# Row maxima turned in blocks by VectorE and DMA, an earlier front and masks first, in a two-layer attention kernel

## What is computed

```python
# block 0, with H = 32 heads of D = 16
xn = _layernorm(x)
qkv = xn @ qkv_w + qkv_b                      # 512 -> 3 * 512
q, k = _rope(q, cos, sin), _rope(k, cos, sin)
scores = einsum('bhqd,bhkd->bhqk', q, k) * scale + (1 - causal) * MASK_VAL
s = (softmax(scores) @ v) @ out_w + out_b
g = silu(xn @ W_gate.T) * (xn @ W_up.T) @ W_down.T      # 512 -> 1376 -> 512
x = x + s * silu(g)
# block 1
xn = _layernorm(x)
s = recurrent net of width 64 (4 layers: long convolution, mlp of 256), 512 -> 64 -> 512
g = silu(oct(xn, w_gate)) * oct(xn, w_up), through oct(., w_down)   # ternary octonion weights
x = x + s * silu(g)
```

## Time and profile before

| what | value |
|---|---|
| time, median of 3 runs (lowest to highest) | 611.6 us (611.2 to 612.4) |
| time of the profiled execution | 611.91 us |
| its span | 610.0 us |
| granted TensorE clock, mean | 1.000 |
| busy: PE, PEld | 590.7 us (97%), 424.7 us |
| busy: DVE, ACT, POOL | 383.0, 290.2, 386.2 us |
| DMA | 83.63 MB, 137 GB/s in the mean |

### The profile page before, as it was taken

One profiled execution on the slowest core, in us unless ns is written; L12 is line 12 of the kernel. 1 busy time (PEld: TensorE's weight loads), 2 busy tenths in 40 slices (PEclk: granted clock), 3 DMA queues, 4 the chain that ended last, 5 costly groups with the idle time before them and its releaser, 6 DMA issues.

```text
span 610.0 us, 9847 instructions
## 1 busy us (share of the span) xinstructions
PE 590.7 (97%) x3368; PEld 424.7 (70%) x3368; DVE 383.0 (63%) x912; ACT 290.2 (48%) x448; POOL 386.2 (63%) x598
## 2 busy tenths in 40 slices
PE   6999999999999999999999999999999999999996
PEld 5876666666677887666666666788887676767664
DVE  5986778666427489877786663366985261516257
ACT  3625777556734622276766566354122453232432
POOL 6896956656435578878575555348979594821363
PEclk9999999999999999999999999999999999999999
DMA  9788776654512237658577554942600000000002
GB/s 302 236 303 251 208 212 189 195 139 103 145 54 87 87 103 220 210 165 250 148 216 223 154 160 130 353 157 95 238 5 1 1 0 2 0 1 1 0 30 109
DMA packets 60369, 83.63 MB, mean 137 GB/s; under 512 B 17936, under 2 KB 26768, under 8 KB 60320
## 3 DMA queue, kind: packets, MB, share of 16 engines
q1 hardware_dynamic: 57968, 75.02, 41.2%
q10 hardware_dynamic: 2352, 8.00, 3.4%
HBM read 65.17 MB, written 26.99 MB: 151 GB/s over the span
## 4 chain that ended last, share of the span: by engine, by line
PE 79%; DMA 5%; DVE 3%; issue 3%; POOL 3%; ACT 3%; SPq 2%; POOLq 0%; ACTq 0%; DVEq 0%
PE proj_ps L1004 9%; PE proj_ps L1006 7%; PE proj_ps L1005 7%; PE ctx_ps L1161 5%; PE score_ps L1034 4%; PE proj_ps L1209 4%; PE proj_ps L1210 3%; PE scoreT_ps L1043 3%; PE score_ps L1004 2%; PE score_ps L1006 2%; PE score_ps L1005 2%; PE scoreT_ps L1004 2%; PE scoreT_ps L1006 2%; PE scoreT_ps L1005 2%; PE ctx_ps L1209 2%
## 5 line engine op out<-in xcount | busy, mean ns | idle before, releaser
L821 POOL TENSOR_TENSOR w_lo<-raw,w_hi 128x512 fp32r<-128x512 f32 x98 | 132.3, 1355 | 64.7 <-ACT w_hi L1374 59.2
L1555 DVE CUSTOM_DVE_ANT_0 score_ps<-score_ps,causal 128x512 f32<-128x512 f32 (+3 forms) x256 | 118.9, 522 | 60.7 <-PE score_ps L1034 60.5
L1423 ACT ACTIVATE probs_T<-scoreT_ps 128x1024 f32<-128x1024 f32 x80 | 82.2, 1027 | 46.1 <-PE scoreT_ps L1043 45.0
L1004 PE MATMUL proj_ps<-xn_hi,w_hi 128*128 128x512 f32 x224 | 96.8, 432 | 1.6 <-ACT by_sin L1352 1.2
L1006 PE MATMUL proj_ps<-xn_lo,w_hi 128*128 128x512 f32 x224 | 88.5, 395 | 0.0
L1005 PE MATMUL proj_ps<-xn_hi,w_lo 128*128 128x512 f32 x224 | 88.5, 395 | 0.0
L852 POOL TENSOR_SCALAR_AFFINE_SELECT probs_T<-probs_T 128x256 f32<-128x256 f32 x128 | 55.5, 457 | 14.2 <-ACT probs_T L1423 14.1
L1004 PEld LDWEIGHTS proj_ps<-xn_hi,w_hi 128*128 128x128 f32 x224 | 42.0, 188 | 26.6 <-issue 14.4
L1333 ACT ACTIVATE q_st<-one_turn_ps 2x512 fp32r<-2x512 f32 x64 | 37.5, 587 | 32.5 <-PE one_turn_ps L1020 32.1
L979 POOL TENSOR_TENSOR hsL<-hidden_T,hsH 128x256 fp32r<-128x256 f32 x44 | 37.6, 872 | 23.4 <-ACT hsH L1495 22.9
L1006 PEld LDWEIGHTS proj_ps<-xn_lo,w_hi 128*128 128x128 f32 x224 | 42.2, 188 | 10.0
(11 more groups left out here) (317 smaller groups left out, 1348.6 us busy)
## 6 DMA issues: line engine op xcount, KB each, us to landing
raw<-w SPq DMA_DIRECT2D x98, 256.0 KB, 2.8
rows<-rows_hi SPq DMA_DIRECT2D x32, 256.0 KB, 3.8
arranged<-tern SPq DMA_DIRECT2D x96, 85.0 KB
q_st<-rows SPq DMA_DIRECT2D x32, 200.0 KB
k_st<-rows SPq DMA_DIRECT2D x32, 200.0 KB
rows<-rows_lo SPq DMA_DIRECT2D x16, 256.0 KB, 4.3
gate_w<-arranged ACTq DMA_DIRECT2D x4, 704.0 KB, 7.2
up_w<-arranged ACTq DMA_DIRECT2D x4, 704.0 KB, 8.3
```

The costliest lines, as they stand in the source:

```text
L821: nc.gpsimd.tensor_tensor(w_lo[n % SPLIT][:, :], raw[n % RAW][:, :], F32(w_hi[n % SPLIT][:, :]), ALU.subtract).then_inc(unit_ready, 1)
L1004: nc.tensor.matmul(acc, lh, rh, start=first, stop=False)
L1423: nc.scalar.activation(probs_T[g % 2][x][:, :, :], scoreT_ps[:, :, :], ACT.Exp, scale=0.25).then_inc(probs_ready, 1)
L1555: m = nc.vector.tensor_tensor_reduce(out=block, in0=block, in1=causal[:, S - w:], scale=1.0, scalar=-3e38, op0=ALU.add, op1=ALU.max, accum ...
```

## The change

**Maxima.** POOL's `join_maxima`, PE's `max_turn` and ident_r go. Max_cols becomes one buffer of 32 columns for each query tile. DVE now does for each pair `round_maxima` (a CAST 128x4x2) behind the row maxima of tasks 2 and 4, `rest_of_maxima` (TENSOR_TENSOR 128x4x2) at the end of the slot before the turn, and `turn_maxima` (four STREAM_TRANSPOSE of 32 partitions each, in blocks of 32x32) behind the row maxima of tasks 3 and 0. ACT's two copies become two DMAs of 2x512 elements, issued by ACT, from max_rows to q_st. `scores_T` waits for them (`max_stored`), and so does DVE's next `turn_maxima`, since there is one max_rows.

**Fill.** `deal` no longer holds 22 for a max turn, and its bound is 215 in place of 230. The number of triples over all slots stays. Slots 15, 20, 25, 38 and 41 get one more, slots 14, 23, 24, 39 and 42 one fewer.

**Front.** The ones of V are set in three parts, and PE's 15 matmuls of no use wait for the first part alone. DVE adds eps; ACT centres and scales row tile 3 (two ACTIVATEs, between them the rounding of unit 0's weights). The first unit runs its eight products of xn_hi first, then the four of xn_lo.

**Masks.** On POOL, `keep_causal` stands first in a slot, ahead of the partings of weights and rows.

```diff
 def deal():
-    held = [43 * (score_in(s) is not None) + 33 * (prob_in(s) is not None) + 22 * (max_in(s) is not None) + 53 * (ctx_in(s) is not None)
+    held = [43 * (score_in(s) is not None) + 33 * (prob_in(s) is not None) + 53 * (ctx_in(s) is not None)
...
     for s in range(SCORE_SLOTS):
         room += length - held[s]
-        while len(at) < TRIPLES and (room >= triple / 2 and at.count(s) < 3 or held[s] + triple * at.count(s) < 230):
+        while len(at) < TRIPLES and (room >= triple / 2 and at.count(s) < 3 or held[s] + triple * at.count(s) < 215):
             k = len(at)
...
 RAW, SPLIT = 4, 5
-WARM = 10
+WARM = 15
 COPIES = (50, 49)
...
-    ident_r = sb("ident_r", [P, P], f32r)
...
-    at[0] += E * 4
+    max_rows = sb("max_rows", [32, S], f32)
     out_bias = sb("out_bias", [P, E], f32)
...
-    max_cols = sb("max_cols", [P, 2, NT, 34], f32r)
+    max_cols = sb("max_cols", [P, NT, 32], f32r)
...
-            nc.gpsimd.memset(V[:, :, :], 1.0).then_inc(ones_set, 1)
+            nc.gpsimd.memset(V[:, 0, 0:P], 1.0).then_inc(ones_set, 1)
+            nc.gpsimd.memset(V[:, 0, P:], 1.0).then_inc(ones_set, 1)
+            nc.gpsimd.memset(V[:, 1:, :], 1.0).then_inc(ones_set, 1)
...
-            def join_maxima(b, j):
-
-                pool.wait_ge(part_ready, TASKS * b + PARTS * (j // 2) + (3, 5)[j % 2])
-                if PAIRS * b + j == 0:
-                    pool.wait_ge(cols_set, 1)
-                if PAIRS * b + j >= 2:
-                    b0, j0 = divmod(PAIRS * b + j - 2, PAIRS)
-                    pool.wait_ge(turned, use(b0, ("max", j0)) + 1)
-                maxima = row_max[:, j % 2, :].rearrange("p (t h) -> p t h", t=NT)
-                hi, lo = (max_cols[:, j % 2, :, x:34:32] for x in range(2))
-                nc.gpsimd.tensor_scalar(hi, maxima, 1.0, 0.0, ALU.mult, ALU.add).then_inc(max_hi, 1)
-                pool.wait_ge(max_hi, PAIRS * b + j + 1)
-                nc.gpsimd.tensor_tensor(lo, maxima, F32(hi), ALU.subtract).then_inc(max_ready, 1)
...
                 pair = slice(2 * x, 2 * x + 2)
-                pool.wait_ge(mv_ready, 2 * x + 2)
-                nc.gpsimd.tensor_scalar(var_eps0[:, pair], mean_var[:, pair, 1], EPS, 1.0, ALU.add, ALU.mult).then_inc(eps_added, 1)
                 pool.wait_ge(eps_added, x + 1)
                 nc.gpsimd.tensor_tensor(rstd[:, pair], var_eps0[:, pair], half[:, 0:2], ALU.pow).then_inc(rstd_ready, 1)
             for b in range(B):
...
-                        pool.wait_ge(xn_ready, NT)
+                        pool.wait_ge(xn_ready, NT - 1)
                     split(u0 + u)
                     if b == 0 and u == 1:
-                        nc.gpsimd.memset(F32(max_cols[:, :, :, :]), 0.0).then_inc(cols_set, 1)
+                        nc.gpsimd.memset(F32(max_cols[:, :, :]), 0.0).then_inc(cols_set, 1)
                 if b:
                     pool.wait_ge(out_used, KC * b)
                     nc.gpsimd.memset(V[:, :, :].rearrange("p t (h c) -> p t h c", c=32)[:, :, :, D:], 1.0).then_inc(ones_set, 1)
                 rope_lo(b, Q_UNIT[0])
...
-                    if max_in(s) is not None:
-                        join_maxima(b, max_in(s))
+                    if s and prob_in(s - 1):
+                        keep_causal(b, s - 1)
                     for u in split_in_slot(s):
                         split(u0 + u)
                     for u in rest_in_slot(s):
                         rope_lo(b, u)
-                    if s and prob_in(s - 1):
-                        keep_causal(b, s - 1)
...
-            def max_turn(b, j):
-                pe.wait_ge(max_ready, PAIRS * b + j + 1)
-                if PAIRS * b + j == 0:
-                    pe.wait_ge(ident_rounded, 1)
-                n = use(b, ("max", j))
-                if TURN_BANK[n][1]:
-                    pe.wait_ge(turn_done(n), TURN_BANK[n][1])
-                for qt in range(NT):
-                    m = nc.tensor.matmul(turn_bank(n)[0:34, qt * P:(qt + 1) * P], max_cols[:, j % 2, qt, :], ident_r[:, :], start=True, stop=True)
-                m.then_inc(turned, 1)
...
+                pe.wait_ge(xn_ready, NT * (k + 1) - 1)
                 for kc in chunks:
...
+                pe.wait_ge(*((xn_ready, t + 1) if t < NT - 1 else (last_scaled, 1)))
                 for kc in range(KC):
                     m = nc.tensor.transpose(turn_bank(norm_use(0, kc))[:, t * P:(t + 1) * P], xn_first[:, t, kc * P:(kc + 1) * P], ident[:, :])
                     if t == NT - 1:
                         m.then_inc(turned, 1)
+            def first_job():
+
+                wh, wl = unit(0, 0)
+                pe.wait_ge(unit_ready, 1)
+                for kc in range(KC):
+                    c = slice(kc * P, (kc + 1) * P)
+                    pe.wait_ge(xh_ready, kc + 1)
+                    nc.tensor.matmul(first_ps[0], wh[:, c], xn_hi[:, kc, :], start=kc == 0, stop=False)
+                    nc.tensor.matmul(first_ps[0], wl[:, c], xn_hi[:, kc, :], start=False, stop=False)
+                for kc in range(KC):
+                    n0 = norm_use(0, kc)
+                    pe.wait_ge(*turn_released(n0))
+                    m = nc.tensor.matmul(first_ps[0], wh[:, kc * P:(kc + 1) * P], xn_lo[:, kc, :], start=False, stop=kc == KC - 1)
+                m.then_inc(proj_done, 1)
+
             for b in range(B):
                 for u in (Q_UNIT[0], K_UNIT[0]):
+                    if b == 0 and u == 0:
+                        first_job()
+                        continue
                     for kc in range(KC):
                         if u == 0:
...
+                            pe.wait_ge(max_stored, 32 * (PAIRS * b + 2 * g + x // 2 + 1))
                         if s > LAG:
                             pe.wait_ge(probs_ready, TASKS * b + s - LAG)
...
-                    if max_in(s) is not None:
-                        max_turn(b, max_in(s))
...
-                n, g = use(b, ("max", j)), GROUPS * b + j // 2
-                act.wait_ge(turned, n + 1)
+                n, g = PAIRS * b + j, GROUPS * b + j // 2
+                act.wait_ge(max_turned, n + 1)
                 for hh in range(2):
-                    m = nc.scalar.activation(q_st[g % 3][64 * hh:64 * hh + 2, j % 2, :], turn_bank(n)[32 * hh:32 * hh + 2, :], ACT.Copy)
-                m.then_inc(turn_done(n), 1)
+                    act.dma_start(F32(q_st[g % 3][64 * hh:64 * hh + 2, j % 2, :]), max_rows[2 * hh:2 * hh + 2, :]).then_inc(max_stored, 16)
...
-            for u in range(2):
-                split_hi(u)
+            act.wait_ge(mean_ready, 1)
+            nc.scalar.activation(xn_first[:, NT - 1, :], X[:, NT - 1, :], ACT.Identity, bias=mean_neg[:, :]).then_inc(last_centred, 1)
+            split_hi(0)
+            act.wait_ge(last_centred, 1)
+            act.wait_ge(rstd_ready, 2)
+            nc.scalar.activation(xn_first[:, NT - 1, :], xn_first[:, NT - 1, :], ACT.Copy, scale=rstd[:, NT - 1:NT]).then_inc(last_scaled, 1)
+            split_hi(1)
             norm_hi(0)
...
-                act.wait_ge(ones_set, 2 + b)
+                act.wait_ge(ones_set, 4 + b)
...
+            def round_maxima(b, j):
+
+                n = PAIRS * b + j
+                maxima = row_max[:, j % 2, :].rearrange("p (t h) -> p t h", t=NT)
+                hi = max_cols[:, :, 0:4:2]
+                dve.wait_ge(part_ready, TASKS * b + PARTS * (j // 2) + (3, 5)[j % 2])
+                if n == 0:
+                    dve.wait_ge(cols_set, 1)
+                else:
+                    dve.wait_ge(max_turned, n)
+                nc.vector.tensor_copy(hi, maxima).then_inc(max_hi, 1)
+
+            def rest_of_maxima(b, j):
+
+                n = PAIRS * b + j
+                maxima = row_max[:, j % 2, :].rearrange("p (t h) -> p t h", t=NT)
+                hi, lo = (max_cols[:, :, x:4:2] for x in range(2))
+                dve.wait_ge(max_hi, n + 1)
+                nc.vector.tensor_tensor(lo, maxima, F32(hi), ALU.subtract).then_inc(max_ready, 1)
+
+            def turn_maxima(b, j):
+
+                n = PAIRS * b + j
+                dve.wait_ge(max_ready, n + 1)
+                if n:
+                    dve.wait_ge(max_stored, 32 * n)
+                for r in range(NT):
+
+                    m = nc.vector.transpose(max_rows[:, :].rearrange("p (t r i) -> p r t i", t=NT, r=4)[:, r], F32(max_cols[32 * r:32 * r + 32, :, :]))
+                m.then_inc(max_turned, 1)
+
...
                 first_stats(t)
-            for t in range(NT):
+                if t % 2:
+                    pair = slice(t - 1, t + 1)
+                    dve.wait_ge(mv_ready, t + 1)
+                    nc.vector.tensor_scalar(var_eps0[:, pair], mean_var[:, pair, 1], EPS, None, ALU.add).then_inc(eps_added, 1)
+            nc.vector.tensor_scalar(mean_neg[:, :], mean_var[:, NT - 1, 0:1], -1.0, None, ALU.mult).then_inc(mean_ready, 1)
+            for t in range(NT - 1):
                 first_rows(t)
             norm_lo(0)
-            dve.wait_ge(ident_in, 16)
```

(8 more changed lines are left out.)

## The result

The changed kernel took 653.07 us in the median (652.49 to 655.15, 4 runs) against 611.4 (611.02 to 612.4, 4 runs) for the kernel before: a ratio of 1.0685, with a 95% interval of 1.0658 to 1.0712. It is 42 us slower. The forecast was 609.0, with a range of 604.5 to 616.5, and the most likely case had the wrong sign.

What follows compares the result with a forecast made beforehand. PE, busy 97% of the span, was taken to bound the kernel. 13.1 us off its list, 10.1 of them given back, made -3.0: 611.9 to 608.9, said as 609.0, range 604.5 to 616.5.

Steps and rivals of the forecast that it cites:

- The turns leave PE, 13.1 us gross: PE's list in attention: 7.4 for turns, 4.0 bank, 1.2 masks and 0.5 exp waits, 13.1 us off in all.
- slot walk: All attention slots stepped through with three start rules for scores, row maxima and banks; 10.1 of 13.1 us come back, net -3.0.
- the bank's wait: Eight turns start late until DVE has read the sums from the same PSUM bank; 0.50 each, 4.0 us saved.
- the masks' 1.2: PE waits for masks behind partings of weights at slot 21, once in each batch; masks first saves 1.2 us.
- The front, 0: Kernel start: first product near 11.1 instead of 12.37, but slot 5 still waits for k_st; bounds -1.3 to +0.3, taken 0.
- What DVE gets, 1.0 and 0.2: Per pair on DVE: four transposes 1.0 us, rounding and rest 0.2 each; 45 us over 32 pairs.
- +6.6: The whole sum in us, in place of -3, if a set of four transposes on DVE took about 1.4 us.
- rival C: DVE's transposes run one after another, small operations slowed beside GpSimd: +2 to +10 us, mainly 614 to 618; chance 0.24.
- The landing, 2.0 us: The two 4 KB DMAs of maxima land in 2.0 us before the transposed scores, with 1.8 to 2.5 left; costs 0.4.
- Rival D: The 4 KB DMAs of maxima wait among SP's transfers; at a landing of 2.8 us +2, 614 us; chance 0.16.
- A: The forecast itself: PE's gain in attention mostly given back by DVE; -3, 607 to 611 us; chance 0.38.
- B: DVE's additions fit its gaps, or the front's 1.3 us is real: -6 to -8, 604 to 607 us; chance 0.22.

Runs made afterwards that it cites:

- the kernel with both edits: Changed kernel with one transpose of four for all pairs but the first, and nothing waiting for the maxima's DMAs (maxima left out): 601.76 us, ratio 0.9831.
- the swap of two blocks: Kernel before, with VectorE reading the turned sums ahead of the slot's row maxima instead of behind them: 608.25 us, ratio 0.9942.
- the kernel of 621.8: Changed kernel with the maxima's DMAs writing to unused rows and PE's transposed scores not waiting for them: 621.82 us, ratio 1.0139.
- two orders that hid the landing: Changed kernel with triples ahead of PE's transposed scores, first only in slots that wait for the maxima (642.76 us), then in every slot (663.27 us).

## Why the prediction was wrong, point by point

**What bounds the kernel.** Right as far as it went: PE's list bounded it, and it did get shorter. It left out that behind new waits of PE the clock can fall from the upper level, where it had been throughout attention, and that this costs nearly as much again as the idle time.

**The turns leave PE, 13.1 us gross.** Right, as far as the runs can tell. My slot walk, fed with the measured 0.3 us for one transpose, 0.32 and 0.37 for the small ones and no landing, gives -9.7; the kernel with both edits measured -10.3. The 4.0 us of the bank's wait showed as 3.4 by the swap of two blocks, the masks' 1.2 as 1.3.

**The front, 0.** Right in the sum. In after the first product starts at 11.59 (forecast 11.1, before 12.37):

```profile
11.59 0.47 PE L1067 MATMUL score_ps<-xn_hi,w_hi 128*128 128x512 f32 x1 [0.45 <-ACT xn_hi L1317]
```

and with it in place the time did not move (608.14 to 608.04 us), as the chain of the earlier trace rows said.

**What DVE gets, 1.0 and 0.2.** Too small, inside the bounds that were given. The groups of after:

```profile
L1582 DVE STREAM_TRANSPOSE max_rows<-max_cols 32x128 f32<-32x128 f32 x128 | 38.3, 299 | 2.7 <-DMA q_st<-max_rows 1.3
```

The set takes 1.24. The trace agrees with the rule of the Trainium skill that was weighed (VectorE: DVE Perf Modes, "Two Vector instructions with no wait between them"): each transpose starts from another 32 partitions, and each waits for the end of the one before, 0.31 start to start with a duration of 0.30. No run has two transposes that start from the same partitions, so whether the change of partitions is the reason stays open. The estimate from the same page's "The three transpose paths", 1.4, was nearer than my 1.0, in part by luck: the page's 311 ns are for 128x128 in bf16, and these are 32x128 in float32. The sum that I gave for it, +6.6, does not follow from my own 1.6 us for each 0.1, which makes +3.4. I had chosen 1.0 by the row of 128x128 in the earlier trace rows, though the other two rows there said that such a change of partitions costs the whole duration. The small operations measured 0.32 and 0.37 in the mean of the kernel in which PE does not wait for the landing, and in one timeline of after, once beside GpSimd's work and once without:

```profile
122.66 0.40 DVE L1564 CAST max_cols<-row_max 128x8 fp32r<-128x8 f32 x1
...
128.00 0.17 DVE L1564 CAST max_cols<-row_max 128x8 fp32r<-128x8 f32 x1
```

The walk with 1.24, 0.32 and 0.37 gives +3.8 where the kernel of 621.8 measured +9.8. So rival C was right about the mechanism, and the +9.8 lies inside its +2 to +10; it is the walk with the measured sizes that is 6 us short. Some 3 of these lie in slot 6 of the first batch, where that kernel takes 6.8 us against 3.0, with the clock at its lower level for 3.4. And there the landing is at work after all: VectorE's set waits for the DMAs of the pair before, and PE then waits for VectorE.

```profile
56.58 1.24 DVE L1582 STREAM_TRANSPOSE max_rows<-max_cols 32x128 f32<-32x128 f32 x4 [1.22 <-DMA q_st<-max_rows]
58.68 0.76 PE L990 MATMUL proj_ps<-xn_hi,w_hi 128*128 128x512 f32 x1 [2.26 <-DVE hidden_T L1636]
```

The rest is open.

**The landing, 2.0 us.** This is the step that failed: the term of 2.0 us, priced at 0.4 us of time. The nearest rows were of large DMAs from a quiet stretch (1.7 us) and of a median (2.8). The forecast counted from the end of the second issue. Counted so, the 19 pairs with no stack load in flight landed in 1.1 us in the median (up to 2.5), the other 13 in 4.1 (3.2 to 4.7). The issues took 0.57 each in place of 0.4 and the set 1.24 in place of 1.0, which took 0.6 of the 1.8 to 2.5 us that were left. PE's wait for it measured 27.3 us, and without that wait the kernel is 31.3 us faster. The 8.29 us of k_st's transfer stood in the earlier trace rows, and that SP issues it in the same slots could be read in the code; the deadline was worked out correctly and then held against the median. By the walk a landing of 5.0 us for every pair costs 28 us, and I had priced it only up to 3.5. Rival D named the mechanism, with a chance of 0.16 and a price of +2.

**The clock.** No term of the sum, and no rival. Of the 31.8 us of the landing (by the spans) about 15 are the clock's, 30.7 us more at the low level at half speed, and about 17 are time in which PE stands still. But not every wait is followed by a fall: of the 16 waits for the landing in after nine are (1.3 to 3.4 us long), seven are not (0.3 to 1.7).

**Chances.** A and B together had 0.60 and both rested on a landing that stays under the deadline. C and D were taken as apart, though both could hold at once; what happened was both.

## What to carry to other kernels

Price a small DMA on a path that others wait for by the transfers that are in flight when it is issued, not by its size and not by the median of landings: here two DMAs of 4 KB took 2.3 to 3.8 us from the first issue without, and 4.3 to 6.0 with, the four loads of 200 KB in flight. When a wait of PE is created and PE bounds the kernel, add what its clock loses: here 15 us on top of 17. And before work is moved off the bounding engine, look for why it stood late there: the swap of two blocks that frees the PSUM bank earlier gave 3.4 us.

## What the runs showed that I had not expected

- PE's order inside a slot cannot be turned without its partners' lists: two orders that hid the landing (1.9 and 3.5 us of waits left) opened 15 and 37 us of waits for ACT and VectorE.
- Behind nine waits for the landing of 1.3 to 3.4 us PE ran at its lower level, eight times for 3.4 us and once for 10.2, though it was busy again at once. The kernel before, with waits of under 1 us there, has no such stretch. In the kernel with both edits PE waited 2.67 us for k_st at 39 us and stayed at the upper level, so the length of one wait does not decide it alone.
- A VectorE operation of 8 columns took 0.17 us or 0.40, in the same kernel and 5 us apart.
